# A memset and a wait behind each row scatter on GpSimd, in a routed FFN kernel

## The reference, cut to what matters

```python
# x: (16, 512, 512); 8192 tokens of 512 numbers in 16 batches
y = gelu(x @ W.T + fc_bias + (x @ v / 512) @ u.T / 16 + b)      # per batch: low rank term from v = u, row b
prob = softmax(y @ w_router + b_router)                          # 16 blocks ("experts")
idx = top_k(prob, 4)
h = relu(einsum('nd,ebd->neb', y, w1b) + b1b)                    # each expert: 128 hidden units
ffn = einsum('neb,ebd,ne->nd', h, w2b, mask) + b2                # only the 4 chosen experts count
out = x + ffn
```

## Time and profile before

| | |
|---|---|
| median of 3 runs | 1310.8 us (1292.05 to 1319.59) |
| span of the profiled execution | 1288.1 us |
| PE busy | 911.6 us (71%) |
| DVE busy | 828.0 us (64%) |
| ACT busy | 584.8 us (45%) |
| POOL busy | 584.3 us (45%), 589 instructions |
| mean granted clock of TensorE | 0.869 |
| software DMA queue (POOL's) | 27.0% of 16 engines, 136.37 MB |
| hardware DMA queue (SP's) | 49.6%, 217.21 MB |

### The profile page before, as it was taken

One profiled execution on the slowest core, in us unless ns is written; L12 is line 12 of the kernel. 1 busy time (PEld: TensorE's weight loads), 2 busy tenths in 40 slices (PEclk: granted clock), 3 DMA queues, 4 the chain that ended last, 5 costly groups with the idle time before them and its releaser, 6 DMA issues.

```text
span 1288.1 us, 17916 instructions
## 1 busy us (share of the span) xinstructions
PE 911.6 (71%) x4924; PEld 702.2 (55%) x4924; DVE 828.0 (64%) x1964; ACT 584.8 (45%) x1061; POOL 584.3 (45%) x589
## 2 busy tenths in 40 slices
PE   8887789889899998888898774898898981000000
PEld 7664567677677766666676553677676761000000
DVE  4444355666556665556656563877687867987777
ACT  5434345565556555465546453765566560000000
POOL 1455664555565655555565655454455543000000
PEclk9988789989999999999999896999999996555555
DMA  5777577776787777777876765787888759999999
GB/s 173 266 241 272 190 245 278 263 258 228 252 272 264 252 263 256 246 259 242 269 261 235 254 237 220 239 261 236 288 271 259 232 166 357 414 429 429 426 430 385
DMA packets 103234, 354.82 MB, mean 275 GB/s; under 512 B 29961, under 2 KB 29961, under 8 KB 92384
## 3 DMA queue, kind: packets, MB, share of 16 engines
q1 hardware_dynamic: 59104, 217.21, 49.6%
q0 software_dynamic: 43936, 136.37, 27.0%
q10 hardware_dynamic: 96, 0.10, 0.0%
HBM read 200.47 MB, written 169.65 MB: 287 GB/s over the span
## 4 chain that ended last, share of the span: by engine, by line
PE 46%; another core or an unknown queue 13%; DMA 12%; DVE 11%; issue 8%; ACT 7%; ACTq 2%; DVEq 1%; POOL 0%; POOLq 0%; SPq 0%
PE yps L1201 10%; DMA w2l<-yt 10%; PE lay L1068 9%; PE trn L1158 8%; PE hid L1173 7%; PE hid L1178 4%; DVE gsb L744 3%; PE hid L1054 3%; PE trn L1088 2%; DVE stx L935 2%; ACT gsb L578 2%; DMA outT<-ys 2%; ACTq L589 1%; PE rps L1103 1%
## 5 line engine op out<-in xcount | busy, mean ns | idle before, releaser
L744 DVE TENSOR_TENSOR gsb<-trn,gsb 128x512 fp32r<-128x512 f32 x286 | 192.0, 687 | 258.3 <-ACT gsb L578 216.5
L498 POOL DMA_INDIRECT yt<-ys,ids x218 | 235.2, 1079 | 244.9 <-ACT ys L637 177.3
L472 POOL DMA_INDIRECT xg<-grow,ix x224 | 221.4, 988 | 139.6 <-DVE ix L818 74.2
L1158 PE MATMUL trn<-idf,gr 128*128 128x128 f32 x1144 | 185.6, 287 | 106.4 <-DVE gsb L744 101.1
L1158 PEld LDWEIGHTS trn<-idf,gr 128*128 128x128 f32 x1144 | 140.3, 146 | 170.1 <-DVE gsb L744 135.8
L1068 PE MATMUL lay<-w2l,xs 128*128 128x512 f32 x768 | 201.7, 414 | 0.0
L578 ACT ACTIVATE gsb<-trn 128x512 fp32r<-128x512 f32 x286 | 171.6, 600 | 30.1 <-PE trn L1158 16.5
L1068 PEld LDWEIGHTS lay<-w2l,xs 128*128 128x128 f32 x768 | 151.4, 201 | 33.1
L606 ACT ACTIVATE hv<-hid,b1c 128x512 f32<-128x512 f32 (+1 forms) x94 | 52.6, 584 | 222.6 <-PE hid L1178 106.8
L1201 PE MATMUL yps<-w2c,hh 128*128 128x512 f32 x368 | 140.6, 465 | 6.2 <-issue 4.5
L1173 PE MATMUL hid<-gsb,w1c 128*128 128x512 f32 (+1 forms) x576 | 133.2, 374 | 8.0 <-issue 7.8
(11 more groups left out here) (184 smaller groups left out, 1518.4 us busy)
## 6 DMA issues: line engine op xcount, KB each, us to landing
gr<-xg SPq DMA_DIRECT2D x49, 1056.0 KB
xs<-yt SPq DMA_DIRECT2D x16, 2048.0 KB, 19.5
w2l<-yt SPq DMA_DIRECT2D x15, 2048.0 KB, 19.7
gr<-xg SPq DMA_DIRECT2D x45, 528.0 KB
stx<-xT SPq DMA_DIRECT2D x64, 256.0 KB, 4.2
outT<-ys SPq DMA_DIRECT2D x31, 512.0 KB, 20.4
xg<-xrow SPq DMA_DIRECT2D x16, 528.0 KB
w2f<-xrow SPq DMA_DIRECT2D x16, 512.0 KB
```

The source lines that it names most:

```text
L472: pool.indirect_dma_start(out=xg, out_offset=bass.IndirectOffsetOnAxis(ap=ix[:, row_buffer(b), q, k:k + 1], axis=0), in_=grows[row_buffer( ...
L498: pool.indirect_dma_start(out=yt, out_offset=bass.IndirectOffsetOnAxis(ap=ids[:, j % 8, c:c + 1], axis=0), in_=yss[result_buffer(j)][:, c, ...
L744: dve.tensor_tensor(gsb[:, :, LO, c * P:(c + 1) * P], trn[n % 2][:, :].rearrange("p (k t) -> p k t", k=KC), gsb[:, :, HI, c * P:(c + 1) * ...
L1158: last = pe.transpose(trn[n % 2][:, k * P:(k + 1) * P], gr[:, j % 2, c, k * P:(k + 1) * P], idf[:, :])
```

## The change

A helper `rest()` is added on POOL. It sets a tile `pace` of 16 floats per partition to zero, increments the new semaphore `g_pace` with it, and waits for that increment. It is called after each of the 256 row scatters (L472 before, L482 after), so four times in each call of `place_rows`. The sends of results (L498) and the writes of the table (L483, L488) are left as they are. Nothing is taken out and no other engine's program is changed.

```diff
+        pace = sb("pace", [P, 16], F32)
...
-        g_z, g_id, g_up, g_tok, g_k, g_s = (sem(n) for n in ("g_z", "g_id", "g_up", "g_tok", "g_k", "g_s"))
+        g_z, g_id, g_up, g_tok, g_k, g_s, g_pace = (
+            sem(n) for n in ("g_z", "g_id", "g_up", "g_tok", "g_k", "g_s", "g_pace"))
...
+            paced = [0]
+
+            def rest():
+
+                pool.memset(pace[:, :], 0.0).then_inc(g_pace, 1)
+                paced[0] += 1
+                pool.wait_ge(g_pace, paced[0])
+
             def place_rows(b, q):
                 pool.wait_ge(v_ix, b + 1)
...
                 for k in range(TOPK):
                     pool.indirect_dma_start(
                         out=xg, out_offset=bass.IndirectOffsetOnAxis(ap=ix[:, row_buffer(b), q, k:k + 1], axis=0),
                         in_=grows[row_buffer(b)][:, q, :], in_offset=None).then_inc(s_sc[row_buffer(b)][q], 16)
+                    rest()
```

## The result

The changed kernel takes 1216.2 us as the median of four runs (1214.39 to 1220.94), the kernel before 1309.5 us beside it: a ratio of 0.934, 95% interval 0.924 to 0.943. That holds for the runs of this comparison.

The account below looks back on a forecast made before the run. No engine full; PE leads at 71% and idles because its semaphore increments arrive late behind POOL's DMA chains. 1288.1 - 60 (middle) - 5 (early) = 1223 us, as a median (factor 1.018) 1245; range 1200 to 1350.

Parts of the forecast that it names:

- Bound and delay: While POOL issues DMAs back to back, PE's increments arrive late, about 1 us after the chain ends; `hidden` starts 3.1 us late.
- the tests named ahead: Signs of being right: L606 "remote" waits under 30 us, PE idle under 40, L637 wait under 1 us a step, step 13.2.
- A chain of four or fewer does little: On POOL, a chain of up to four DMAs hardly delays PE's increments, a long one much.
- A spacing of 1.56 is above that: Each scatter seemed to need about 0.1 us more than 1.26 us; a 0.3 us rest, spacing 1.56, would be enough.
- early stage: POOL's 26.1 us a batch bind; with some wait for `ix` 27.5 us, over five batches 5 us less.
- middle stage: A step is held by PE's 12.6 or POOL's 12.75 us, taken as 13.2 against 14.74; 39 steps, 60 us less.
- The factor 1.018: Median of runs over profiled execution before, 1310.8 / 1288.1, used to turn the predicted 1223 us into 1245.
- The price of a rest: Time each rest adds between two scatters on POOL: 0.3 us likely, lower bound about 0.05, upper about 1.0.
- the dear rest: Rival: a rest costs about 1 us, so POOL binds middle steps and early batches; median 1388 us, chance 0.09.
- The estimate of 1.2 us behind the last DMA: PE's increments come through 1.23 us after the last DMA of a chain of seven on POOL.
- The delay stays and the chain gets longer: Rival: release still comes about 1.2 us after the last scatter, which ends 1.2 us later each step; median 1383, chance 0.14.
- Nothing: Rival: POOL's longer list, at about 0.6 us a rest, eats the gain of earlier semaphores; median 1306 us, chance 0.15.

Follow-up runs that it names:

- the late wait: Changed kernel with POOL's wait for each memset moved to just ahead of the next memset: 1317.1 us, ratio 1.008 to the kernel before.
- the first set: Four follow-up kernels with varied rests, beside the kernel before at 1305.5 us; in the second set, twelve minutes later on the same chip, before took 1123.2 us.
- the third experiment: Changed kernel with two rests in place of one behind every row scatter: 1238.6 us, ratio 0.949 to the kernel before.

## Why the prediction was right, and where it was off

**Bound and delay: right, in the condition that it was made for.** PE's increments came late behind POOL's chains, and in this condition the rests set them free. Of the tests named ahead: L606's waits against "remote" to under 30 us: 13.9. PE idle in the middle under 40 us: 43.5 in the stretch shown, just missed, and 34.6 over the 40 steps in which before has 71.0. POOL's wait for L637 under 1 us a step: 55.2 us in 550, or 43 steps of 12.8, is 1.3, missed. The middle step from 14.74 to 13.2: from 14.6 to 13.0 in the steady part. The inference that the chain is the cause was half of it: the chain has a part, since taking it apart removes much of the delay, but so has something outside the program that the traces don't show. By which mechanism a chain of POOL holds back increments of PE stays unknown.

**"A chain of four or fewer does little": not borne out.** The changed kernel still has chains of four sends. All scatters on their own took back 75 of the 167 us that the delay costs; the early stage, where each scatter rests, is still 23 us longer than without the delay (185.6 against 162.6). An increment that fell inside a DMA came through at its end, as at 511.07 above.

**"A spacing of 1.56 is above that": not shown.** The prediction reckoned that about 0.1 us more between two scatters is enough. The spacing became 1.37 us, and 128.8 of 229.0 us of waits against "remote" are still there. In the early stage it took the second rest, at some 1.7 us a scatter, to end them.

**The sum, term by term.**

| term | predicted | measured |
|---|---|---|
| early stage | -5 | -15.1 |
| middle stage | -60 | -50.0, and -7.8 at the last row scatters |
| late tiles and closing | 0 | -2.1 |
| from the profiled span to the median | +22 | +3 |
| total | 1245 | 1216 |

*The factor 1.018* is the largest miss. The profiled execution of before was faster than its median, and I carried that over as if it belonged to the program. The runs of after lie within 0.5%, those of before within 2.1%; with the delay went most of the spread between runs, and median and profiled execution fall together (1216.2 and 1213.1).

*The price of a rest*, taken at 0.3 us, is 0.2: ahead of a scatter POOL stands (71.3 + 27.0) / 254 = 0.39 us on the mean against 74.5 / 242 = 0.31 before, plus 0.127 for the memset. The guess that the memset would begin 0.2 to 0.3 us after the DMA was wrong, it begins at once; the lower bound of 0.05 was nearly right for most rests (0.10). The rival of the dear rest falls: with the wait the next scatter starts 0.28 us after the memset, without it 0.18 us, so the wait itself costs 0.1 us. The Trainium skill's rule that completion needs all eight cores (GPSIMD Engine Reference, "Instruction dispatch") may hold, but behind a row scatter it has no price beyond that; nor has the shared port ("Key points" there), with a median scatter of 968 ns against 960 and memsets of 125 to 143 ns.

*The middle stage* was summed with two terms that are off. POOL's 11.55 us a step hold 1.02 us in which it waited for ACT between two sends, 0.7 us more than a plain gap. And PE's 12.6 us a step were taken at the clock of before: PE's busy time for the 40 steps fell by 13.6 us as the clock rose, and without the delay a step takes 12.06 us of PE. The saving by a higher clock is no term of the sum.

*The early stage* got a batch of 25.7 us, (171.9 - 43.2) / 5, and not 27.5: POOL's own need, but for one wait of 3.8 us for `ix`. That doesn't explain the whole stage. Without the delay the changed kernel needs 24.7 us a batch, nearly the same, and reaches the first `hidden` 23 us sooner.

*The late gain* was not in the working at all. From step 67 on POOL places rows ahead of its sends, so that sends, table and scatters form one chain, 29 DMAs from 753.20 us on. In the kernel before it ends like this:

```profile
789.90 0.96 POOL L472 DMA_INDIRECT xg<-grow,ix  x1 [0.30 <-issue]
...
794.55 0.69 ACT L606 ACTIVATE hv<-hid,b1c 128x512 f32<-128x512 f32 x1 [18.23 <-remote]
```

ACT had stood for 18.2 us. DMA bandwidth can hardly be the reason, since the DMA engines are half idle while PE, DVE and ACT do nothing:

```profile
784.00:788.00 4.00, 0.00 (x0) 0.00 (x0) 0.00 (x0) 0.00 (x0) 3.08 (x4) 0.50 0.52 205
```

The estimate of 1.2 us behind the last DMA was read from chains of seven; behind this one, of 29, it is 3.7 us. In the changed kernel a chain of sends and tables is left at this place, and ACT still waits 6.03 us there against "remote".

**The rivals.** "The delay stays and the chain gets longer" is what the late wait shows on a small scale, 1.008 instead of the 1.056 it was priced at, since its spacing did not grow. "Nothing" was priced for a gain that POOL eats up; what the runs without the delay show, 1.018, is a plain loss with nothing to gain. That the whole gain hangs on a condition outside the program was in no rival, and that the comparison was made while it held was luck.

## What to carry to other kernels

Where an engine starts later than the matmul that it waits for has ended, and the profile puts the wait down to "remote", look at what GpSimd issues in that time: a chain of indirect DMAs may hold the increments back, and a memset with a wait for it behind each row scatter, about 0.2 us each, gave back 75 of 167 us here. It must fit into GpSimd's time: behind the sends it cost about 0.6 us each, and more than it gave. Measure on more than one occasion before keeping it: the same edit gave 0.934 and 1.018, and the kernel before took 14% less time in one set of runs than in another. A second chip is not a second occasion by itself, since one and the same chip had both. Compare stages by marks that count the work (the n-th tile), not by marks on the engine that the change moves.

## What the runs showed that was not expected

- The same program took 1310 and 1122 us, with equal durations of DVE, ACT and POOL instructions and an equal closing stage. The difference of 167 us between the two traces lies, but for 1.3 us ahead of the first scatter and 0.5 us in the closing stage, where POOL issues indirect DMAs while PE works. What makes it is not known; chip number 7 had it in the first set and not in the second.
- With the delay one wait of 18.23 us held three engines, with the DMA share at 0.52.
- Something shows on SP's queue as well. A register move on SP's queue (here before, then the same program without the delay) keeps within 29 to 43 ns in every trace without the delay; its longest is 686 to 1377 ns in those with it:

```profile
L337 SPq MOVE gr<-xg x94: 3/35/699, 181.0 to 1044.3; - x94
```

```profile
L337 SPq MOVE gr<-xg x94: 29/35/43, 138.2 to 878.7; - x94
```

- A memset right behind an indirect DMA starts with no gap at all, and the next scatter follows 0.18 us after it without a wait, 0.28 with one; a send follows 0.78 us after it.
- Open: whether the wait is needed or 0.1 us of spacing is enough; how the gain divides by stage when rests are left out; and whether two rests behind each early scatter and one behind the later ones add to the change, as the 5.5 us of the third experiment suggest.
